# A two-kind attention and mixture kernel: a reordered start and end, a spread scatter, padded output weights, and the mixture's fourth projections moved to slot 1 of the following pass

## The reference

```
x = x + attn_a(norm(x)); x = x + mix(norm(x)); x = x + attn_b(norm(x)); x = x + mix(norm(x))

attn:  16 heads of 8; q, k, v projections with bias; rotary on q and k;
       causal softmax(q k^T / sqrt(8)) v; output projection with bias
mix:   8 heads of 64; q = x Wq, k = x Wk (128 x 512 each)
       v[t,h] = sum over 5 experts e of (top 2 of x Ws)[t,h,e] * sigmoid * (x Wv[e])
       attn = softmax(q k^T / 8) v, no mask
       out = sum over h, e of (top 2 of x Wd)[t,h,e] * attn[t,h] @ Wo[e]
```

## Time and profile before

| what | value |
|---|---|
| median of 3 runs | 2039.72 us (2038.28 to 2042.88) |
| profiled execution | 2036.81 us, its span 2035.1 us |
| busy: PE, DVE, ACT, POOL | 88%, 77%, 63%, 52% of the span |
| chain that ended last | PE 65%, DVE 16%, ACT 8%, POOL 6% |
| granted TensorE clock | 0.97 of full speed over the span |
| passes 3 to 15 | 116.57 us each |

### The profile page before, as it was taken

One profiled execution on the slowest core, in us unless ns is written; L12 is line 12 of the kernel. 1 busy time (PEld: TensorE's weight loads), 2 busy tenths in 40 slices (PEclk: granted clock), 3 DMA queues, 4 the chain that ended last, 5 costly groups with the idle time before them and its releaser, 6 DMA issues.

```text
span 2035.1 us, 32651 instructions
## 1 busy us (share of the span) xinstructions
PE 1788.4 (88%) x11328; PEld 891.2 (44%) x11328; DVE 1572.6 (77%) x2934; ACT 1279.3 (63%) x2803; POOL 1057.5 (52%) x1124
## 2 busy tenths in 40 slices
PE   1658999989999998999999898999999899998775
PEld 0223444545445354544545454544545454454332
DVE  4527888788888888888888878888888888887461
ACT  0235757576675867667585767667576766758462
POOL 1123656374655637374664637465573646555433
PEclk8778999999999999999999999999999999999877
DMA  3231312112120311213120211213031121200000
GB/s 98 49 37 33 37 30 36 21 43 32 43 38 30 44 36 27 30 38 37 43 38 30 35 22 41 34 43 37 30 43 35 26 32 38 37 19 12 11 1 6
DMA packets 87617, 68.71 MB, mean 34 GB/s; under 512 B 10720, under 2 KB 83104, under 8 KB 87328
## 3 DMA queue, kind: packets, MB, share of 16 engines
q1 hardware_dynamic: 87456, 66.62, 17.8%
HBM read 32.51 MB, written 10.49 MB: 21 GB/s over the span
## 4 chain that ended last, share of the span: by engine, by line
PE 65%; DVE 16%; ACT 8%; POOL 6%; issue 2%; DMA 2%; SPq 0%; POOLq 0%; DVEq 0%; ACTq 0%; PEldq 0%
PE Y L463 12%; PE M L556 5%; PE S2a L428 5%; POOL Z L1074 5%; PE S1c L404 5%; ACT Pq L688 4%; PE S2b L428 4%; DVE nmaxF L853 4%; PE S1b L404 3%; PE M L593 3%; PE Y L454 3%; PE M L514 3%; DVE nmaxA L848 2%; DVE ztmp L935 2%; PE M L567 2%
## 5 line engine op out<-in xcount | busy, mean ns | idle before, releaser
L1074 POOL TENSOR_TENSOR Z<-Z,ztmp 128x1280 f32<-128x1280 f32 x112 | 324.7, 2899 | 335.8 <-DVE ztmp L963 334.7
L1041 POOL TENSOR_SCALAR_AFFINE_SELECT PT<-PT 128x256 f32<-128x256 f32 (+1 forms) x640 | 264.4, 424 | 347.4 <-ACT PT L673 342.7
L1065 POOL TENSOR_TENSOR Vf<-Vf,ztmp 128x512 f32<-128x512 f32 x256 | 349.5, 1365 | 101.8 <-DVE ztmp L935 93.2
L673 ACT ACTIVATE PT<-S2a 128x512 f32<-128x512 f32 x320 | 191.7, 599 | 125.1 <-PE S2a L422 118.7
L463 PE MATMUL Y<-PT,Vf 128*64 128x512 f32 x1024 | 267.8, 614 | 0.0
L677 ACT ACTIVATE PT<-S2a 128x512 f32<-128x512 f32 x256 | 153.1, 598 | 147.9 <-PE S2a L428 145.2
L935 DVE TENSOR_TENSOR ztmp<-xv,wv_s 128x512 f32<-128x512 f32 x256 | 237.6, 928 | 2.8 <-POOL Z L1074 2.8
L404 PE MATMUL S1c<-Kf,Qf 64*128 64x512 f32 x352 | 202.6, 656 | 31.7 <-ACT Pq L688 29.7
L404 PE MATMUL S1a<-Kf,Qf 64*128 64x512 f32 x352 | 201.7, 653 | 31.4 <-ACT Pq L688 31.4
L673 ACT ACTIVATE PT<-S2b 128x512 f32<-128x512 f32 x320 | 191.7, 599 | 39.0 <-PE S2b L422 38.7
L404 PE MATMUL S1b<-Kf,Qf 64*128 64x512 f32 x320 | 182.8, 652 | 13.9 <-ACT Pq L688 12.0
(11 more groups left out here) (108 smaller groups left out, 3744.8 us busy)
## 6 DMA issues: line engine op xcount, KB each, us to landing
Qs<-parts SPq DMA_DIRECT2D x96, 128.0 KB
Ks<-parts SPq DMA_DIRECT2D x96, 128.0 KB
tab_s<-in_tab SPq DMA_DIRECT2D x16, 512.0 KB, 4.3
xr<-out_x SPq DMA_DIRECT2D x32, 256.0 KB, 2.9
out_x<-res SPq DMA_DIRECT2D x32, 256.0 KB, 2.5
wa_s<-in_wa SPq DMA_DIRECT2D x16, 320.0 KB, 3.1
xl<-out_x SPq DMA_DIRECT2D x16, 256.0 KB, 3.0
out_x<-in_x SPq DMA_DIRECT2D x8, 256.0 KB, 4.5
```

What stands on the lines that cost most here:

```text
L673: nc.scalar.activation(PT[:, slot % 2, b, :], t[:, :], ACT.Exp, scale=SCALE_A).then_inc(exps_done.sem, 1)
L1041: last = nc.gpsimd.affine_select(out=v, in_=v, compare_op=ALU.is_ge, fill=0.0, base=0, pattern=pattern, channel_multiplier=-1)
L1065: nc.gpsimd.tensor_tensor(Vf[:, i, :, :], Vf[:, i, :, :], vtmp[:, n % VBUF, :, :], ALU.add).then_inc(v_acc.sem, 1)
L1074: nc.gpsimd.tensor_tensor(Z[:, :, :, :], Z[:, :, :, :], ztmp[:, hh % 2, :, :, :], ALU.add).then_inc(z_acc.sem, 1)
```

## The change

It has these parts.

1. Start: x is no longer copied to the output; the first round reads x from the input (`stream_in`), loads in the queue first the two small constants, then the first x and attention weights, then the mixture's weights under a semaphore of their own. `Qs` and `Ks` are cleared by VectorE in pass 0 ahead of slot 2 and the ones written ahead of slot 4.
2. Scatter: each of the six DMAs fills 8 partitions that lie 4 apart (`rows_of`), so the parts occupy 48 of the first 64 rows, in another order.
3. `ZT` has memory of its own; `Z` and the third chunk of the output weights are padded with zeros to 128, so that its three chunks are equal.
4. `F q3` and `F k3` are projected at (1, 6) of the next pass, with `f` instead of `f_prep`, and their places in the bank lists move.
5. In pass 17 (`UNITS + 1`) the transposes of `Z` and the output move to (3, 9) and (4, 1), and each head's first score matmul waits for its own bank alone.

```diff
+    def rows_of(r):
+        return slice(32 * (r // 4) + r % 4, 32 * (r // 4) + r % 4 + 4 * (DA - 1) + 1, 4)
-    ZCH = [(0, 128), (128, 256), (256, NX)]
+    ZCH = [(0, 128), (128, 256), (256, 384)]
-        Z = sb("Z", [P, NT, E, DF])
+        Z_wide = sb("Z", [P, NT, E + 1, DF])
+        Z = Z_wide[:, :, 0:E, :]
+        ZT = sb("ZT", [P, 3, T])
-        ZT = parts[:, :, :, :].rearrange("p q c t -> p (q c t)").bitcast(F32).rearrange("p (c t) -> p c t", c=3)
         M0_USES = ["rows1",
-                   "rows2", "ZT1", "F out",
+                   "rows2", "F k3", "ZT1", "F out",
...
-                   "rows0", "F k2", "F k3"]
+                   "rows0", "F k2"]
         M1_USES = ["YT6",
-                   "YT7", "ZT0", "ZT2",
+                   "YT7", "F q3", "ZT0", "ZT2",
...
-                   "YT5", "F q2", "F q3"]
+                   "YT5", "F q2"]
-        F_STEPS = [(6, 8), (6, 9), (7, 6), (7, 8)]
+        F_STEPS = [(6, 8), (6, 9), (7, 6), (1, 6)]
+        def steps_of_output(k):
+            return ((3, 9), (4, 1)) if k == UNITS + 1 else ((1, 9), (2, 1))
...
-            for b in range(B):
-                sp.dma_start(out[b], x[b]).then_inc(x_copied.sem, 16)
...
-            sp.wait_ge(x_copied.sem, 16 * B)
-            sp.wait_ge(dve_init.sem, dve_init.per)
+            def stream_in(u):
+                return (x if u < B else out)[u % B].rearrange("(t p) c -> p t c", p=P)
...
+                if j == 0:
+                    sp.dma_start(wqk_s[:, :], wqk).then_inc(weights_loaded.sem, 16)
+                    sp.dma_start(wgv_s[:, :], wgv).then_inc(weights_loaded.sem, 16)
...
                         for r in range(NSP):
-                            sp.dma_start(dst[DA * r:DA * r + DA, :, :],
+                            sp.dma_start(dst[rows_of(r), :, :],
                                          parts[:, qk, order[r], :]).then_inc(scattered.sem, 16)
...
-                        pe.wait_ge(*drained(j, "F q3", 1))
-                        pe.wait_ge(*drained(j, "F k3", 1))
-                    pe.wait_ge(*s1_free(j, (n if group < SA else n + 1) - len(S1)))
+                        pe.wait_ge(*drained(j, "F q2", 1))
+                        pe.wait_ge(*drained(j, "F k2", 1))
+                    if group == SA + 3 and b == 0:
+                        pe.wait_ge(*drained(j, "F q3"))
+                        pe.wait_ge(*drained(j, "F k3"))
+                    alone = group >= SA and j == UNITS + 1
+                    pe.wait_ge(*s1_free(j, (n if group < SA or alone else n + 1) - len(S1)))
...
+                            if alone and h:
+                                pe.wait_ge(*s1_free(j, n + h - len(S1)))
...
-                        if not f_prep:
+                        if not (f_prep if p < 3 else f):
...
-            nc.vector.memset(Qs[:, :, :], 0.0).then_inc(dve_init.sem, 1)
-            nc.vector.memset(Ks[:, :, :], 0.0).then_inc(dve_init.sem, 1)
...
+            nc.vector.memset(Z_wide[:, :, E, :], 0.0).then_inc(dve_init.sem, 1)
+            nc.vector.memset(wo_s[NX - 256:P, 2, :], 0.0).then_inc(dve_init.sem, 1)
...
+                    if j == 0 and slot == 2:
+                        for rows in (Qs, Ks):
+                            nc.vector.memset(rows[0:ROWS_P1, :, :], 0.0).then_inc(rows_zeroed.sem, 1)
+                    if j == 0 and slot == SA:
+                        nc.vector.memset(Ks[ROWS_P1:ROWS_P2, :, :], 1.0).then_inc(ones_ready.sem, 1)
```

More of the change, by code:

```diff
@@ L248, in is_free, with place, free_for @@
             return (m0_drained if use in M0_USES else m1_drained).sem
+        def place(k, use):
+            uses = M0_USES if use in M0_USES else M1_USES
+            if k == UNITS + 1:
+                late = [u for u in uses if u in ("ZT0", "ZT1", "ZT2", "F out")]
+                uses = [u for u in uses if u not in late]
+                first = uses.index("A yNT" if "A yNT" in uses else "YT2")
+                uses = uses[:first] + late + uses[first:]
+            return uses.index(use)
         def filled(k, use, lag=0):
-            uses, signal = (M0_USES, m0_filled) if use in M0_USES else (M1_USES, m1_filled)
-            return signal.sem, signal.at(k, uses.index(use) + 1, lag)
+            signal = m0_filled if use in M0_USES else m1_filled
+            return signal.sem, signal.at(k, place(k - lag, use) + 1, lag)
         def drained(k, use, lag=0):
[L256 to L261, removed]
+            signal = m0_drained if use in M0_USES else m1_drained
+            return signal.sem, signal.at(k, place(k - lag, use) + 1, lag)
+        def free_for(k, use):
+            signal = m0_drained if use in M0_USES else m1_drained
+            return signal.sem, signal.at(k, place(k, use))
+        def steps_of_output(k):
+            return ((3, 9), (4, 1)) if k == UNITS + 1 else ((1, 9), (2, 1))
         def s1_free(k, n):
@@ L415, in pass2 @@
                         return
+                    if b == 0 and slot == 0:
+                        pe.wait_ge(ones_ready.sem, 1)
                     if b == 0 and slot < SA:
@@ L750, in iteration @@
                             drain("F xnT", xnT[:, :], bank("F xnT")[:, :])
-                        if at in F_STEPS and f_prep:
+                        if at in F_STEPS and (f_prep if slot > 5 else f):
                             f_copies(F_STEPS.index(at))
@@ L758, in iteration @@
                             f_gates(3)
-                        if at == (1, 9) and f_end:
+                        if at == z_step and f_end:
                             for c in range(3):
                                 lo, hi = ZCH[c]
-                                if c == 0:
-                                    act.wait_ge(scattered.sem, scattered.at(j, 0))
                                 drain(f"ZT{c}", ZT[0:hi - lo, c, :], bank(f"ZT{c}")[0:hi - lo, :])
@@ L1014, in iteration @@
                             f_value_product(*divmod(V_STEPS.index(at), E))
-                        if at == (2, 1) and f_end:
+                        if at == out_step and f_end:
                             f_output()
```

37 lines of the change are left out of this document (21 added, 16 removed).

## The result

The changed kernel takes 1959.28 us (median of 4 runs, 1956.49 to 1961.99), the kernel before 2041.3 in the same session (4 runs, 2038.28 to 2046.78): ratio 0.959, 95% interval 0.9577 to 0.9603. The forecast was 1959 (1940 to 1990), faster. The profiled execution took 1957.9, the one before 2036.81, so 78.9 us less in the traces; the sum had 80.9.

The account below looks back on a forecast made before the run. Bounds differed by stretch: init work and scatter, scatter again, TensorE or VectorE by slot, GpSimd's sums then bank loop. 27.8 + 12.5 + 1.0 + 23.8 + 15.8 = 80.9 off 2036.81 gives 1955.9; plus 2.9, 1959 (1940 to 1990).

Parts of the forecast that it names:

- Head: Start to first score matmul: an earlier start and faster scatter landing move it from 66.22 to 38.4, saving 27.8 us.
- Second pass: Pass after the head: scores no longer stand 15.41 us for the scatter; 12.5 us saved, then normalisation is late.
- Pass 2: The pass without mixture output yet: 1.0 us saved.
- The middle: Passes 3 to 16: moved projections and shorter mixture output save 1.7 us a pass, 23.8 in all.
- The move: Fourth projections from slot 7 to next pass's slot 1: TensorE keeps 0.7 of its 1.5 us, VectorE all.
- VectorE doesn't see it: Slot 1: TensorE's lateness from the moved projections misses VectorE, which is in gapless work of its own into slot 2.
- The padding: Mixture output in slot 2: 24 passes with all weights on 128 rows cost 2.7 us, 1.4 saved.
- Tail: Pass 17 to the end: new order, single banks and shorter output save 10, 2.5 and 1.5; together 15.8 us.
- A: Rival for head and second pass: the scatter is no faster, taking back 13.5 and 12.5; 1985 us, chance 0.16.
- B: Rival for the middle: it gives nothing, slot 1 late as slot 7 is early; 1983 us, chance 0.15.
- C: Rival, slower: TensorE stands in slot 1 for the last mixture product's bank, 5.1 us a pass; 2061 us, chance 0.05.
- D: Rival: A and B together, half the tail's and head's gains lost; within 4 us of now; chance 0.03.

Follow-up runs that it names:

- e11: The changed kernel with the scatter's query and key rows on neighbouring partitions again: 1987.39 us, ratio 0.9725.
- e2: The kernel before with only the scatter's destination rows spread four apart: 2018.78 us, ratio 0.9877.
- e1: The changed kernel with the fourth pair's projections at their old place, (7, 8) of their own pass: 1977.64 us, ratio 0.9672.
- e4: The changed kernel with pass 17 in its old order (transposes, output, score matmuls waiting for a pair of banks): 1972.0 us, ratio 0.9649.
- e7: The changed kernel with single banks in pass 17 only in slots 2 and 3: 1956.61 us, ratio 0.9573.
- e10: The changed kernel with four extra matmuls filling TensorE's wait for the fourth queries' bank in pass 17: 1963.44 us, ratio 0.9606.
- e12: e9 with two more TensorE waits filled, by eight matmuls in pass 17's slot 2 and sixteen before the last output: 1953.37 us, ratio 0.9557.
- e8: The changed kernel with the fourth keys projected before the fourth queries: 1956.73 us, ratio 0.9572.
- e3: The kernel before with only Z and the third chunk of output weights padded to 128: 2026.13 us, ratio 0.9918.
- e9: e8 with three extra matmuls in pass 17 filling TensorE's wait for the fourth queries' bank: 1957.2 us, ratio 0.9575.
- e5: The changed kernel with the scatter's rows two apart instead of four: 1960.18 us, one execution.
- e6: The changed kernel with the scatter's rows eight apart instead of four: 1966.22 us, one execution.

## Why the prediction was right, and where it only came out right

**Head: right in mechanism and size.** 29.9 for 27.8. The statistics start at 5.35, not 6.5, the rotation at 17.62 (18 forecast), and the flight after the last issue is 2.9, the fast end of the range, not 4. The fill with ones is hidden. e11 and e2 split it: 14.9 by the start (14.4 forecast), 15.1 by the rows (13.4).

**Second pass.** 14.6 for 12.5, with the named next wait, the normalisation. The scatter is not waited for at all, as forecast. The 2.1 more are not settled: the forecast left out that the fourth projections no longer stand at the end of this pass, and e1, with them, has 82.80. But in the traces of the kernels with the changed kernel's code up to there (e4, e7 to e10, e12) this pass takes 77.24 to 79.89, so a difference of 2 us is no more than their spread.

**Pass 2.** 1.0 slower, not 1.0 faster (112.08 for 111.11). Slot 7 gave its 1.8, slot 2 took 1.4 more (19.59 for 18.20). Small, wrong in sign. It goes with the rows: slot 2 is 19.35 in e2, which has nothing but them, and 18.42 in e11, which has all but them. What differs is the granted clock of that slot, 0.83 for 0.91; the forecast had no clock there. How the rows bring it about stays open.

**The middle: right in mechanism, both terms too high.** 1.47 a pass for 1.7. The move was taken at 0.7 on TensorE and 1.5 on VectorE; e1 shows 0.59 for the pass. The step that failed is "VectorE doesn't see it": slot 1 grew by 1.07, not by 0.5 at most, and VectorE pays in slot 2, where it stands 0.26 and 1.37 for the mixture's score banks. With TensorE's stand of 0.48 taken away (e8) these waits are 0 and 0.97 and the pass is 0.60 shorter, so TensorE's lateness was on the path. The padding was taken at 1.4 and saved TensorE that (4.24 to 2.89), but gives the pass only 0.87 (e3), near the 0.80 by which VectorE's waits in slot 2 became shorter (0.47 and 1.29 before, 0.96 in e3). The discount from the sum of both, 2.1, to 1.7 was right in direction and too small.

**Tail: the sum is right, its terms are not.** 17.4 from the start of pass 16 on, for 17.5 forecast (the 15.8 and one pass of 1.7). That is luck. To GpSimd's last sum 0.9 were saved (3.5 forecast: both the projections' 1.8 and the pass's 1.7 end in a wait for GpSimd). From there to slot 4 it was 15.9, not 10, at the upper end of the range given (4 to 16). Slots 4 and 5 became 1.6 longer, not 2.5 shorter; the forecast did not price the output that moves into slot 4. The end gave 2.2 for 1.5, and it loses as much again when the clock is low in the last output (below).

The 15.9 has three parts. The first 3.4 need no new order: from the sum to slot 4 are 35.4 us before, 32.0 in e4 and 32.1 in e3, which has the padding alone. The other 12.5 are the order with the clock that follows from it. With the new order at a clock of 0.50 the last stretch is 50.1 (e8, e9), at 1.00 it is 44.4, in the old order 56.8, at 0.62 in the window shown (e4). So about 6.7 us are the order's and 5.7 the clock's, and the second part can be lost by an edit that has nothing to do with it, as in e1 and e8. The forecast priced a bank from a row at 0.60 and did not ask what the clock would do.

**The whole.** 80.9 forecast and 78.9 measured in the traces: the head, read at the first exponential, and the second pass gave 3.5 more, pass 2 and the middle 5.4 less. The median came within 0.3 of 1959 because the step from the profiled execution to the median, taken as 2.9, was 1.4. So the closeness is partly luck; the range and the mechanisms of the head and the second pass are not.

**Rivals.** A fell (151 to 46 ns, e2, e11). The number of DMA engines, which the rival named, was not the limit: the scatter became faster with the same eight rows a DMA. B fell (1.47 a pass, both parts shown). C fell: the wait at its place is 0.48, and slot 1 grew by 1.07, where 3.7 a pass were needed. D fell with the time.

| part | forecast | measured | shown by |
|---|---|---|---|
| head | 27.8 | 29.9 | e2, e11 |
| second pass (pass 1) | 12.5 | 14.6 | e2, e11, e1 |
| pass 2 | 1.0 | -1.0 | e2, e11 |
| passes 3 to 15 | 22.1 | 18.65 | e1, e3 |
| pass 16 to the end | 17.5 | 17.4 | e4, e7, e8 |

The head is read at the first score matmul; at the first exponential it is 29.2 (79.56 to 50.34), and with that the five parts make the 78.9 of the two traces.

## What to carry to other kernels

When a DMA is slow for its size, look at which partitions it lands on before its count or bytes; a strided destination was worth 25 us here for one line (e2). Price moved work by what stands in its new place on every engine, not only on the one that runs it, and look which of the two banks it writes is free first (e8: 0.6 a pass for swapping two lines). And read the granted clock beside every stretch that follows a wait of TensorE: a gain there may belong to the clock, and an unrelated edit can take it away.

## What the runs showed of the hardware that was not expected

- TensorE took 24 passes with all weights on 128 rows in 2.89 us, and 24 that mix 128 and 64 rows in 4.24. Padding the weights with zeros was faster here than the smaller matmul (e3 has that edit alone).
- The granted clock after a wait of TensorE is not told by that wait alone. After 4.23 us of idling the changed kernel had 0.69 and then 1.00; after 3.20 e8 had 0.50 for 24 us in which TensorE was busy 22.90; with work put into the wait, e9 (0.51) and e10 (0.60) fell after the next one. With the keys first, only the kernel with both waits filled (e12) stayed at 1.00. Why the changed kernel recovers within some microseconds, as do e5, e6, e7 and e11, and e8 does not stays open.
- From the first exponential of pass 17's slot 7 to the end it was 43.42 us in the changed kernel, 43.59 in e7, 45.79 in e6 and 46.09 in e11, which have no edit there. The difference lies between GpSimd's last sum and the end of the output: 6.97 at a granted clock of 0.79 in the first two, 9.35 and 9.47 at 0.52 and 0.51 in the others.
- Packets of 1 KB to rows eight apart took 92 ns, to rows two apart 78.
